# The source row of the fetched edge tile: converted by ScalarE into PSUM, compared by VectorE from there

## The reference, cut to what matters

```python
h = jnp.maximum(_layernorm(x, axis=-1), 0.0)
hW = jnp.einsum('nd,tdf->tnf', h, W_edge) + b_edge[:, None, :]
msg = hW[etypes, src]
seg = dst * T + etypes
counts = segment_sum(ones, seg)
agg = segment_sum(msg / counts[seg][:, None], dst)
out = hN[ntypes, arange(N)] + agg
x = x + relu(out)
```

## Time and profile before

| | |
|---|---|
| median of three runs | 578.05 us |
| the profiled execution, its time | 577.35 us |
| its span in the profile | 575.5 us |
| TensorE busy (matmuls) | 424.4 us, 74% |
| GpSimd busy | 410.4 us, 71% |
| VectorE busy | 363.4 us, 63% |
| ScalarE busy | 172.7 us, 30% |
| mean granted TensorE clock | 0.881 of full speed |

### The profile page before, as it was taken

One profiled execution on the slowest core, in us unless ns is written; L12 is line 12 of the kernel. 1 busy time (PEld: TensorE's weight loads), 2 busy tenths in 40 slices (PEclk: granted clock), 3 DMA queues, 4 the chain that ended last, 5 costly groups with the idle time before them and its releaser, 6 DMA issues.

```text
span 575.5 us, 9581 instructions
## 1 busy us (share of the span) xinstructions
PE 424.4 (74%) x3143; PEld 353.8 (61%) x3143; DVE 363.4 (63%) x913; ACT 172.7 (30%) x402; POOL 410.4 (71%) x384
## 2 busy tenths in 40 slices
PE   0249929796887697688669668869776967686797
PEld 0249817675676476567558557657664856575586
DVE  5965569846764665764665766557656657746743
ACT  1932433413312412421341242133224124303410
POOL 9075088877777777777777777777777777777750
PEclk9999978977987897888788989779878879977989
DMA  6461037423423423433442332333334234423320
GB/s 161 114 158 38 2 65 245 155 65 123 125 65 123 128 65 116 130 87 96 128 129 62 128 125 79 109 123 97 97 120 128 60 118 132 116 73 123 124 49 9
DMA packets 32496, 60.34 MB, mean 105 GB/s; under 512 B 7416, under 2 KB 22836, under 8 KB 29236
## 3 DMA queue, kind: packets, MB, share of 16 engines
q1 hardware_dynamic: 19372, 34.83, 18.5%
q0 software_dynamic: 11776, 24.14, 15.7%
q10 hardware_dynamic: 1296, 0.71, 0.5%
HBM read 56.01 MB, written 3.65 MB: 104 GB/s over the span
## 4 chain that ended last, share of the span: by engine, by line
PE 63%; issue 14%; DMA 13%; DVE 4%; POOL 3%; ACT 1%; SPq 1%; DVEq 0%; POOLq 0%; ACTq 0%
PE acc L690 19%; PE out_ps L337 18%; PE misc L276 11%; DMA G<-h_table,src_t 10%; PE acc L670 5%; PE out_ps L328 5%; POOL G L390 3%; PE node_ps L317 3%; DMA xs<-in_x_dram 2%; PE out_ps L330 1%; ACT union_a L540 1%; SPq L402 1%; PE misc L337 1%; DMA cnt_table<-union_b 1%; DVE union_b L987 1%
## 5 line engine op out<-in xcount | busy, mean ns | idle before, releaser
L390 POOL DMA_INDIRECT G<-h_table,src_t x368 | 396.9, 1078 | 146.1 <-issue 95.1
L690 PE MATMUL acc<-oh,G 128*128 128x384 f16 (+1 forms) x784 | 145.0, 317 | 114.9 <-issue 67.5
L970 DVE TENSOR_TENSOR S<-S,acc 128x384 f32 x196 | 108.2, 552 | 160.4 <-PE acc L690 159.9
L690 PEld LDWEIGHTS acc<-oh,G 128*128 128x128 f16 x784 | 76.9, 104 | 167.4 <-issue 96.7
L337 PE MATMUL out_ps<-w_all,union_a 128*128 128x128 f32 x768 | 124.5, 331 | 0.0
L337 PEld LDWEIGHTS out_ps<-w_all,union_a 128*128 128x128 f32 x768 | 120.8, 247 | 0.8
L961 DVE TENSOR_SCALAR oh<-iota,seg 128x224 f16<-128x224 f16 (+1 forms) x396 | 103.8, 314 | 10.8 <-issue 10.8
L283 ACT ACTIVATE G<-misc 128x256 f16<-128x256 f32 x24 | 9.2, 384 | 271.9 <-PE misc L276 271.9
L276 PE MATMUL misc<-hh,union_c 128*128 128x256 f16 x600 | 78.3, 275 | 0.0
L276 PEld LDWEIGHTS misc<-hh,union_c 128*128 128x128 f16 x600 | 59.0, 99 | 5.6
L309 ACT ACTIVATE S<-zcol 128x2048 f32<-128x2048 f32 x23 | 43.9, 1909 | 59.1 <-DVE union_a L353 59.1
(11 more groups left out here) (97 smaller groups left out, 171.5 us busy)
## 6 DMA issues: line engine op xcount, KB each, us to landing
union_b<-rc_table SPq DMA_DIRECT2D x25, 1024.0 KB, 4.8
G<-h_table,src_t POOLq DMA_INDIRECT x368, 2.6
h_table<-hh SPq DMA_DIRECT2D x5, 320.0 KB, 2.6
src_row<-in_src_dram SPq DMA_DIRECT2D x24, 64.0 KB, 3.0
out_dram<-os SPq DMA_DIRECT2D x24, 64.0 KB
xs<-in_x_dram SPq DMA_DIRECT2D x4, 320.0 KB, 5.2
w_all<-in_L_gnn_W_node_dram SPq DMA_DIRECT2D x1, 512.0 KB
xs<-in_x_dram SPq DMA_DIRECT2D x1, 256.0 KB
```

The source lines that it names most:

```text
L390: nc.gpsimd.indirect_dma_start(out=G[:, slot, :], out_offset=None, in_=h_table[:, :], in_offset=bass.IndirectOffsetOnAxis(ap=index, axis=0 ...
L690: last = nc.tensor.matmul(window[:, :, 0:w], G[:, 2 * g_slot + a, part * D:(part + 1) * D], oh[:, o, a, 0:R * w].rearrange("p (t n) -> p t ...
L970: nc.vector.tensor_tensor(span, span, acc[bank][:, 0:R * W].rearrange("p (t n) -> p t n", n=W), ALU.add).then_inc(s_add, 1)
```

## The change

The conversion of the source row moves from VectorE to ScalarE (`act_row`), which writes it as float32 into 128 columns of the PSUM tile `misc` that were free. VectorE's three compares read the row from PSUM; the node numbers still come from SBUF in float16. Since the row has one buffer, and TensorE's fetch writes another part of `misc`, TensorE now begins the fetch when all three compares are done, and no longer one part at a time. ScalarE does block b + 1's row right behind its copy of block b's fetched tile.

```diff
+        less_mid = sb("less_mid", [P, 1], F32)
-        src_r16 = sb("src_r16", [P, 2, P], F16)
+        row_ps = misc[:, 2 * D:2 * D + P]
+        row_ready = sem("row_ready")
...
+        def act_row(act, b, p, use):
+
+            act.wait_ge(row_in[p], (use + 1) * 16)
+            nc.scalar.activation(row_ps, src_row[:, p, :], ACT.Identity, bias=less_mid[:, 0:1]).then_inc(row_ready, 1)
+            act.wait_ge(row_ready, b + 1)
+            act.sem_inc(row_used, 1)
+
+        def dve_fetch(dve, b, part):
             if part == 0:
-                dve.wait_ge(row_in[p], (use + 1) * 16)
-                nc.vector.tensor_scalar(src_r16[:, p, :], src_row[:, p, :], float(-MID), None,
-                                        ALU.add).then_inc(row_used, 1)
+                dve.wait_ge(row_ready, b + 1)
                 dve.wait_ge(fetch_mm, b + 1)
-                dve.wait_ge(row_used, b + 3)
             first, end = FETCH_PARTS[part]
             nc.vector.tensor_tensor(fetch[:, first:end, :],
-                                    src_r16[:, p:p + 1, :].to_broadcast([P, end - first, P]),
+                                    row_ps.unsqueeze(1).to_broadcast([P, end - first, P]),
                                     node_of[:, first:end, :], ALU.is_equal).then_inc(fetch_oh, 1)
 
         def pe_fetch(pe, b, part):
-            pe.wait_ge(fetch_oh, 3 * b + part + 1)
             if part == 0:
+
+                pe.wait_ge(fetch_oh, 3 * b + 3)
                 pe.wait_ge(fetched, b + 1)
...
+            nc.gpsimd.memset(less_mid[:, :], float(-MID))
...
+                act_row(act, 0, 0, 0)
...
                         act_fetch(act, b)
+                        if b + 1 < 4 * ITERS:
+                            act_row(act, b + 1, (b + 1) % 2, (b + 1) // 2)
```

More of the change, by code:

```diff
@@ L257, in sp_load_row @@
                          ).then_inc(row_in[p], 16)
-        def dve_fetch(dve, b, p, use, part):
+        def act_row(act, b, p, use):
[4 more added lines that the diff above has]
+        def dve_fetch(dve, b, part):
             if part == 0:
-                dve.wait_ge(row_in[p], (use + 1) * 16)
-                nc.vector.tensor_scalar(src_r16[:, p, :], src_row[:, p, :], float(-MID), None,
-                                        ALU.add).then_inc(row_used, 1)
+                dve.wait_ge(row_ready, b + 1)
                 dve.wait_ge(fetch_mm, b + 1)
-                dve.wait_ge(row_used, b + 3)
             first, end = FETCH_PARTS[part]
             nc.vector.tensor_tensor(fetch[:, first:end, :],
-                                    src_r16[:, p:p + 1, :].to_broadcast([P, end - first, P]),
+                                    row_ps.unsqueeze(1).to_broadcast([P, end - first, P]),
                                     node_of[:, first:end, :], ALU.is_equal).then_inc(fetch_oh, 1)
         def pe_fetch(pe, b, part):
-            pe.wait_ge(fetch_oh, 3 * b + part + 1)
             if part == 0:
+                pe.wait_ge(fetch_oh, 3 * b + 3)
                 pe.wait_ge(fetched, b + 1)
@@ L1008, in body @@
                         if v in (1, 2, 3):
-                            dve_fetch(dve, 4 * i + g, g % 2, 2 * i + g // 2, v - 1)
+                            dve_fetch(dve, 4 * i + g, v - 1)
                         add(pair, (u + LATE) % 4, at[u % 4], n0 + done)
```

## The result

The changed kernel takes 575.2 us (median of 20 runs, 569.2 to 579.1), the kernel before 580.5 us (median of 20, 575.6 to 584.0). The ratio is 0.990 (95% interval 0.987 to 0.993): 1.0% faster. Forecast was 573 from 578, a ratio of 0.991. Single executions of either kernel scatter by over 1%, and the one that was profiled first took 579.07 us, the longest of its 20.

What follows compares the result with a forecast made beforehand. GpSimd's unbroken chain of gathers was taken as the bound. Removed holds of -11.8, then +1, +1 and +5 us, sum to -4.8: 577.35 becomes 572.5, or 573 on the median; range 563 to 581.

Steps and rivals of the forecast that it cites:

- holds by compares: GpSimd gathers that begin inside a VectorE compare: their stretch goes when compares read PSUM, 7.5 us in total.
- holds by the conversion: GpSimd gathers that run over VectorE's conversion: 23 stretches of 0.19 us go, 4.3 us in total.
- left from the one-hot in its place: Where the conversion was, the gather meets the one-hot before it: 0 to 0.1 us x 23 stays, taken 1 us.
- block 0, full slots: In block 0 TensorE is 4 us later; GpSimd loses 0 to 2 us once its slots are full, taken 1.
- given back by longer product holds: Gathers beginning inside a product are held 1.54 to 1.64 us, not 1.36: 4.2 to 6.4 us come back, taken 5.
- The compares' length: VectorE's compares from PSUM grow from 0.68 and 0.76 to 1.21 and 1.34 us; VectorE 34 us more in all.
- a sign of being wrong: The prediction is wrong if GpSimd starts to wait for TensorE by more than 0.30 us at a time.
- Only block 0 has no margin: TensorE's fetch has 1.3 us of margin to the third compare, except in block 0, where it starts 4 us later.
- Slower: Rival: the product's hold grows to its greatest, in place of those removed; 580 to 586 us, chance 0.12.
- the compares decide: Rival: TensorE waits for the third compare in each block; about 600 us, chance 0.04.
- Nothing: Rival: TensorE's wait and the product spacings are the true period, 20.4 us a block; 576 to 579 us, chance 0.19.
- Full gain: Rival: the average product hold stays at 1.36 us or less, so nothing is given back; 564 to 569 us, chance 0.20.

Runs made afterwards that it cites:

- after: The changed kernel; its second profiled run, beside the kernel before on one chip, gave ratio 0.989 and a profiled execution of 574.24 us.
- after_prodpsum: Changed kernel whose product multiplies with a constant in PSUM, not the reciprocal counts; on the slower chip 647.1 and 648.0 us, ratios 0.983 and 0.989 to the kernel before.
- after_split4: Changed kernel with each product cut into four instructions of 512 columns: 543.0 us, ratio 0.934 to the kernel before; on the slower chip 647.8 us, 0.988.
- late_fetch: Kernel before, with TensorE's fetch waiting for all three compares: ratio 0.997 (0.994 to 1.000) to the kernel before.
- conv_act: Kernel before, with ScalarE converting the row into SBUF as float16 and compares still reading SBUF: 590.9 us, ratio 1.018 to the kernel before.

## Why the prediction was right

The forecast by its terms, in us, with what the two profiled executions of after measured against the one of before, the second one first:

| term | forecast | measured | in the first execution |
|---|---|---|---|
| holds by compares | -7.5 | -7.5 | -7.5 |
| holds by the conversion | -4.3 | -4.3 | -4.3 |
| left from the one-hot in its place | +1 | +2.1 | +2.0 |
| block 0, full slots | +1 | +2.5 | +2.5 |
| given back by longer product holds | +5 | +4.9 | +7.1 |
| sum, first to last gather | -4.8 | -2.3 | -0.2 |

**What held.** That a second input in PSUM frees the gathers, inferred from 80 additions, is shown by the compares and by after_prodpsum. The compares' length was priced at 1.21 and 1.34 us and is 1.21 and 1.35. VectorE's 32 us more cost TensorE nothing from block 3 on: TensorE waited three times for a compare, in blocks 0 to 2, 6.2 us in all. That the product takes back part of the gain is in the rows of both executions. The reading of before has one slip that changes nothing: 23 gathers begin inside a compare, not 22, and the one at 119.04 begins 0.10 us before the compare's end and takes 0.94.

**What was mis-sized.** Two small terms. In block 0 the fetch began 4.1 us later (92.42 against 88.33), as forecast, but the matmuls behind that wait ran at 1.2 GHz for another 4 us (granted clock 0.50 in the first window below), 1.72 us for eight in place of 1.04. That made TensorE's next sum 5.0 us later than before (96.89 against 91.89), and GpSimd lost 2.5 us and not 1. This wait of 2.79 us is the one that the prediction named as a sign of being wrong; it comes once, in block 0. Timeline, and the windows (busy us and count of each engine, then the granted clock):

```profile
92.42 2.10 PE L284 MATMUL misc<-hh,union_c 128*128 128x256 f16 x9 [3.79 <-DVE union_c L274]
...
95.33 1.72 PE L284 MATMUL misc<-hh,union_c 128*128 128x256 f16 x8
96.34 0.94 POOL L398 DMA_INDIRECT G<-h_table,src_t  x1 [2.79 <-PE acc L702]
...
109.54 1.16 PE L284 MATMUL misc<-hh,union_c 128*128 128x256 f16 x9 [1.21 <-DVE union_c L274]
```

```profile
92.40:96.30 3.90, 3.88 (x18) 2.66 (x19) 2.36 (x8) 0.00 (x0) 0.94 (x1) 0.50 0.95 377
97.00:100.00 3.00, 3.00 (x24) 2.06 (x22) 1.02 (x4) 1.30 (x4) 2.16 (x3) 1.00 0.17 45
```

"Only block 0 has no margin" was too narrow as well: in blocks 1 and 2, where TensorE doesn't wait for rows behind the product, the fetch had to wait too, 1.2 us each (109.54). And the one-hots hold gathers 0.03 to 0.11 us in more places than behind a product; one gather (477.81) met the fold of the ring, another instruction with two SBUF inputs, and lost 0.3.

**The agreement of the total is partly luck.** The profiled pair differs by 3.1 us (574.24 against 577.35), the medians by 5 to 6; the first execution of after was 1.7 us longer than that of before. The one profiled execution of before is itself 3.1 us under the median of its 20 runs. What the rows explain is the pair; the other 2 to 3 us lie within the scatter of single executions, and no row accounts for them. The hold in the products is right on average and not product by product: the prediction took products 17.3, 21.3, 20.7 and 21.8 us apart in turn, and in the first execution they settle at 19.3, 20.4, 20.5 and 21.6, each with a hold of 1.45 to 1.90 us.

**The rivals.** *Slower* and *the compares decide* did not come. *Nothing* took the spacing of the products for the true period; with the product's holds gone too (after_split4) it fell from 19.9 to 18.5 us on average, so it is not TensorE's alone. *Full gain* would need a mean hold at or under 1.36; it was 1.57 and 1.67. The forecast of the product's holds (1.54 to 1.64) was the step that mattered: without it the sum would have been -9.8 us.

**The Trainium skill's inference** that a `tensor_tensor` can't hold the descriptors of a GpSimd DMA, in "SBUF — State Buffer", section "Who interferes with whom", is contradicted for these gathers: 46 held by products in the two runs of after, at up to 2.1 us each, against none from PSUM. The same section's rule, that two SBUF inputs contend with a GpSimd instruction that reads SBUF, fits these rows.

## What to carry to other kernels

An engine whose gaps are all the same small number is the bound, even at 71% busy; sort its instructions by duration and look at what the other engines run when one is long. Here the price of a VectorE instruction was not its own time but what it does to GpSimd's gathers: 32 us more of VectorE for 12 us less of holds was a small gain, since products took 5 to 7 us of it back, and cutting the one long instruction that held most was worth five times as much (0.989 to 0.934) at no cost but 0.2 us a block. When a small hold is removed, ask where the next instruction then begins: with the conversion gone, the compare moved into the same spot and cost four times as much.

## What the runs showed of the hardware

- A gather (indirect DMA by GpSimd, 128 rows, 0.94 us) is held when a VectorE instruction of a holding kind already runs as it starts, and it then ends 0.82 us after that instruction, so one that starts in the instruction's last 0.12 us is not lengthened. At the instruction's start the edge is sharp. In the seven traces with undivided products from SBUF, all 161 gathers that start 0.05 us or more behind a product's start are held (the first of them by 2.12 us), and none of the 5 that start 0.00 to 0.04 us behind it, nor of the 59 that start up to 0.5 us before it. The latest that goes free, in late_fetch:

```profile
481.28 2.37 DVE L353 TENSOR_TENSOR union_a<-S,union_b 128x2048 f32<-128x2048 f32 x1
481.32 0.94 POOL L390 DMA_INDIRECT G<-h_table,src_t  x1 [0.30 <-issue]
```

  What two instructions in a row do at a gather's start is not resolved: a compare from SBUF 0.09 us behind it held all 23 gathers in conv_act, with a one-hot still running; the one at 118.02, 0.10 us behind its gather and with a one-hot too, did not.
- An instruction cut into four lets a waiting gather in between the pieces: 2.29 us became 2.50 us of VectorE, and a mean hold of 1.57 us became 0.09 over the 35 gathers that began inside.
- One chip ran the same kernel 13 to 14% slower (657 to 660 against 581 us), with VectorE and GpSimd instructions as long as elsewhere and TensorE's matmuls issued with unexplained gaps. There the change and the cut together are worth 1.2%, on the first chip 6.6%.
